# Gathers and sums of a graph network: GpSimd's memsets between gathers, and who clears the banks

## The chip, the cores and the metric

The program runs on one core of one Trainium2 chip. The metric is the time of the program on the device in microseconds; less is better. The core's engines are TensorE (PE in the profile, its weight loads PEld), VectorE (DVE), ScalarE (ACT), GpSimd (POOL) and SyncE (SP). Each runs its own stream of instructions, and they meet at semaphores.

## The reference

12500 nodes with 128 features, 212500 edges sorted by destination, each with one of 8 relations. Two relational layers and a third, plain one sum messages over the edges:

```python
def _rgcn_layer(x, W, SW, b, src, dst, rel):
    xt = jnp.einsum('nd,rde->rne', x, W)
    msg = xt[rel, src]
    agg = jax.ops.segment_sum(msg, dst, num_segments=x.shape[0])
    return jax.nn.relu(agg + x @ SW + b)
...
deg = jax.ops.segment_sum(jnp.ones_like(dst, dtype=jnp.float32), dst, num_segments=N)
d_invsqrt = jnp.maximum(deg, 1.0) ** (-0.5)
feat = jax.nn.relu(x @ W1 + b1)
h = feat * d_invsqrt
agg = jax.ops.segment_sum(h[src], dst, num_segments=N)
feat = feat - agg * d_invsqrt
return feat @ W2 + b2
```

Between the layers stand a residual and a layer norm over the features, and another pair at the end. All values are float32.

## The kernel before

Three sums over all edges follow each other: r1 gathers rows of x, r2 rows of x1 (the output of the first layer), r3 rows of h. The edges lie in 1661 **tiles** of 128. For each tile, one indirect DMA on GpSimd's queue (line 794) gathers the 128 source rows of 512 bytes into a slot of `rows`. A one-hot matrix S made by VectorE (line 1042 in r1 and r2, 1235 in r3) says to which of a window's destinations (and, in r1 and r2, relations) each edge belongs, and TensorE multiplies the tile by it (lines 980 and 1205), adding into a PSUM bank.

7 tiles are a **group** (KG) of 64 destinations, two groups a **pair** (PAIR, 14 tiles), four pairs an **iteration** (RING = 8 groups, 56 tiles). `rows` has 56 slots, so the gathers of a pair wait until TensorE is done with the same pair of the iteration before (semaphore `summed`), and until ScalarE has copied their indices (`idx_ready`, line 738). The rest of an iteration's work is for a chunk of 436 nodes whose sums are complete: the classes Tail1, Tail2 and Tail3 (the dense layers, the norms, loads and stores by SyncE).

**GpSimd** (class Gathers, `run`) issues the gathers in order. Behind each it writes a 128x128 MEMSET into a tile `pause` that nobody reads (line 798). The last MEMSET of every group (r1, r2) or of every pair (r3) increments `paused`, and before the next group's (pair's) first gather GpSimd waits for it (line 788). `gate` increments a semaphore that nobody waits for. The first 14 tiles of r2 and 21 of r3 are gathered early (line 764), while the sum before is being finished; these have no MEMSET.

**TensorE** in r1 and r2 (`tensor` in relational_sum): two banks take groups in turn. Group h waits until ScalarE has copied out group h-2 (`agg_out`), clears the bank with a bfloat16 matmul of zeros over its 512 columns (line 964), and adds its 7 tiles. In r1, before the first group of a pair, the matmuls of line 973 count the edges of each destination: 3 for each group, one for each block of 32 destinations that a window of 64 can touch, into 3 columns of 32 rows. VectorE adds these columns to `found` (line 1093). After the first pair of an iteration stands the mix: 8 matmuls of 512 columns (line 950) that multiply the sums of the iteration before, by relation, by the layer's weights. In r3 a group's first matmul starts its bank anew, and there is neither mix nor clearing.

**ScalarE** (`scalar`) copies the indices of the next iteration, waits for the mix, and copies each group out of its bank (`take_out`, line 904); each copy increments `agg_out`:

```python
act.wait_ge(summed, n + (h + 1 + RING))
act.copy(agg[:, h, :, :], agg_ps[h % BUFS][:, :].rearrange("p (n r) -> p n r", r=NREL)
         ).then_inc(agg_out, 1)
```

**VectorE** makes the one-hots two pairs ahead; in r1 also `hot` and `placed` for the counts (lines 1037 and 1040). It adds the mixed sums into `acc` (line 1081), and runs the chunk's elementwise work.

## Time and profile before

| | us |
|---|---|
| median of 3 runs | 7358.1 |
| lowest and highest of them | 7354.17, 7372.18 |
| span of the profiled execution | 7320.2 |
| GpSimd busy | 5851.5 (80%) |
| TensorE busy, matmuls and weight loads | 3691.2 (50%), 2669.6 (36%) |
| VectorE busy, ScalarE busy | 1720.1 (23%), 409.6 (6%) |

The profile comes from one execution, on the core; its own time is not listed apart from its span, which is 37.9 us under the median of the runs. "Busy" counts the time in which an engine executes; waits, branches and register instructions are not in it. For TensorE the ends of matmuls are modelled, so that its busy share is less sure than that of the others. GpSimd's idle time put down to "issue" is time in which no semaphore held it back by the profile: its sequencer and the start of the next instruction. "remote" is a release that the profile could not match with an instruction. The clock is the share of 2.4 GHz that TensorE was granted: 0.5 is 1.2 GHz.

### The profile page before, as it was taken

The page shows a single profiled execution, that of the slowest core. Times are in us where ns is not written, and L with a number is a line of the kernel's source. Part 1 is how long each engine was busy: PE and PEld are TensorE (multiplying, and loading weights), DVE is VectorE, ACT ScalarE, POOL GpSimd, SP SyncE. Part 2 cuts the span into 40 slices and gives each one's busy share as a digit, 9 for nine tenths or more (in the row PEclk, how much of TensorE's full clock was granted, in tenths as well). Part 3 has the DMA queues.
Part 4 walks back from the last instruction along what each step waited for, and adds up shares of the span by engine and source line. Part 5 has one row for each costly group of instructions (what it writes and reads, how often), then busy time and mean ns, then how long its engine had stood idle before and what let it go on. Part 6 is the DMA issues. An engine that isn't in the chain of part 4 may idle for free.

```text
span 7320.2 us, 56431 instructions
## 1 busy us (share of the span) xinstructions
PE 3691.2 (50%) x13687; PEld 2669.6 (36%) x13841; DVE 1720.1 (23%) x2844; ACT 409.6 (6%) x915; POOL 5851.5 (80%) x9940
## 2 busy tenths in 40 slices
PE   4555555555555556556565555554424333433343
PEld 3333333333333333334343333433323333333333
DVE  4333333333333212222222222221101111111111
ACT  1000000000000100000000000010000000000000
POOL 7888888888888588888888888867888888888887
PEclk7666667676666777767677776675555555555555
DMA  2111111111111112211222221211111111111111
GB/s 66 49 51 52 50 50 50 51 52 50 50 52 51 40 49 57 56 56 55 56 58 56 56 57 56 56 54 42 51 51 52 51 51 51 51 51 53 51 51 48
DMA packets 197585, 382.88 MB, mean 52 GB/s; under 512 B 84322, under 2 KB 93326, under 8 KB 197542
## 3 DMA queue, kind: packets, MB, share of 16 engines
q0 software_dynamic: 159456, 326.88, 17.0%
q1 hardware_dynamic: 36416, 54.67, 2.1%
q10 hardware_dynamic: 1670, 0.85, 0.0%
q8 instruction: 15, 0.25, 0.0%
q14 instruction: 28, 0.23, 0.0%
HBM read 356.43 MB, written 25.65 MB: 52 GB/s over the span
## 4 chain that ended last, share of the span: by engine, by line
POOL 48%; issue 20%; another core or an unknown queue 20%; PE 7%; DVE 3%; DVEq 1%; POOLq 0%; ACT 0%; DMA 0%; ACTq 0%; SPq 0%
POOL rows L794 39%; POOL pause L798 9%; PE bank L980 3%; PE bank L950 3%; DVE r_S L1042 1%; DVE r_hot L1037 1%; PE bank L1205 1%; ACT r_agg L904 0%; PE bank L1440 0%; PE bank L964 0%; DVE acc L1081 0%; DMA acc<-in_dst_dram 0%; DVEq L1071 0%; POOLq L109 0%
## 5 line engine op out<-in xcount | busy, mean ns | idle before, releaser
L794 POOL DMA_INDIRECT rows<-in_x_dram,idx x1661 | 1588.6, 956 | 466.9 <-issue 396.7
L794 POOL DMA_INDIRECT rows<-x_d,idx x1647 | 1574.2, 956 | 453.5 <-issue 397.8
L794 POOL DMA_INDIRECT rows<-h_d,idx x1640 | 1566.9, 955 | 441.4 <-issue 396.3
L980 PE MATMUL bank<-r_S,rows 128*128 128x128 f32 x6644 | 1408.2, 380 | 705.1 <-issue 486.8
L1205 PE MATMUL bank<-r_S,rows 128*128 128x64 f32 x3322 | 821.9, 388 | 1332.3 <-issue 1079.4
L980 PEld LDWEIGHTS bank<-r_S,rows 128*128 128x128 f32 x6644 | 1299.5, 285 | 501.4 <-issue 482.1
L1205 PEld LDWEIGHTS bank<-r_S,rows 128*128 128x128 f32 x3322 | 775.1, 315 | 1378.0 <-issue 1272.4
L798 POOL MEMSET pause<- 128x128 f32 x4948 | 1096.3, 222 | 4.3 <-issue 0.2
L1042 DVE TENSOR_TENSOR r_S<-bank,key 128x1792 f32<-128x1792 f32 x238 | 480.4, 2019 | 1225.9 <-remote 1080.3
L964 PEld LDWEIGHTS bank<-zeros_bf 128*128 128x128 bf16 x476 | 54.1, 114 | 1463.0 <-issue 1056.8
L964 PE MATMUL bank<-zeros_bf 128*128 128x512 bf16 x323 | 174.9, 542 | 722.4 <-issue 505.8
L904 ACT COPY r_agg<-bank 128x512 f32<-128x512 f32 x476 | 272.1, 586 | 4257.1 <-remote 3286.7
L1262 DVE TENSOR_TENSOR acc<-acc,bank 128x64 f32 x238 | 52.8, 222 | 1877.3 <-remote 1561.9
L1037 DVE TENSOR_TENSOR r_hot<-bank,b_spot 128x1344 bf16<-128x1344 f32 x119 | 185.4, 1558 | 1223.4 <-remote 1051.5
L950 PE MATMUL bank<-r_agg,w1s 128*128 128x512 f32 (+1 forms) x528 | 459.7, 1036 | 14.3 <-issue 12.7
L950 PE MATMUL bank<-r_agg,w2s 128*128 128x512 f32 (+1 forms) x528 | 458.7, 1035 | 3.7 <-issue 2.0
L1040 DVE TENSOR_REDUCE r_placed<-r_hot 128x192 bf16<-128x1344 bf16 x119 | 289.9, 2436 | 4.1
L950 PEld LDWEIGHTS bank<-r_agg,w1s 128*128 128x128 f32 x528 | 121.9, 234 | 327.2 <-issue 326.3
L950 PEld LDWEIGHTS bank<-r_agg,w2s 128*128 128x128 f32 x528 | 118.3, 225 | 316.4 <-issue 315.4
L1081 DVE TENSOR_TENSOR acc<-acc,bank 128x64 f32 x492 | 109.2, 222 | 406.5 <-PE bank L950 182.7
L973 PE MATMUL bank<-one_bf,r_placed 128*32 128x1 bf16 x714 | 37.5, 168 | 310.5 <-issue 187.3
L1235 DVE TENSOR_TENSOR r_S<-bank,key 128x896 f32<-128x896 f32 x119 | 129.8, 1092 | 35.9 <-DVE acc L1262 22.2
(152 smaller groups left out, 1471.1 us busy)
## 6 DMA issues: line engine op xcount, KB each, us to landing
rows<-in_x_dram,idx POOLq DMA_INDIRECT x1661, 3.3
rows<-x_d,idx POOLq DMA_INDIRECT x1647, 3.4
rows<-h_d,idx POOLq DMA_INDIRECT x1640, 3.4
d_xr<-in_x_dram SPq DMA_DIRECT2D x54, 218.0 KB
x_d<-d_yr SPq DMA_DIRECT2D x27, 218.0 KB
d_x1r<-x_d SPq DMA_DIRECT2D x27, 218.0 KB
h_d<-d_hr SPq DMA_DIRECT2D x27, 218.0 KB
part_d<-d_pr SPq DMA_DIRECT2D x27, 218.0 KB
```

The source lines that it names most:

```text
L794: pool.indirect_dma_start(out=self.c.rows[:, self.place(s), :], out_offset=None, in_=self.table[:, :], in_offset=bass.IndirectOffsetOnAxis ...
L798: ins = pool.memset(self.c.pause[:, s % PT, :], 0.0)
L904: act.copy(agg[:, h, :, :], agg_ps[h % BUFS][:, :].rearrange("p (n r) -> p n r", r=NREL)).then_inc(agg_out, 1)
L950: mm = pe.matmul(mix_ps[:, 0:groups * GN], W[:, r, :], agg[:, first:first + groups, :, r], start=(r == 0), stop=(r == NREL - 1))
L964: pe.matmul(agg_ps[j][:, :], c.zeros_bf[:, :], c.zeros, start=True, stop=False, skip_group_check=True)
L980: mm = pe.matmul(agg_ps[j][:, bass.ds(offs[j * KG + k], TK)], c.rows[:, g.place(h * KG + k), :], S[:, pb, j * KG + k, :], start=False, sto ...
L1037: ch.then(dve.tensor_tensor(hot[:, b, :, :], spots.unsqueeze(1).broadcast_to([P, PT, SPOTS]), bc_last(blocks.spot[:, at], SPOTS), ALU.is_e ...
L1040: dve.tensor_reduce(placed[:, b, :, :], hot[:, b, :, :].rearrange("p (j k) n -> p j n k", k=KG), AX.X, ALU.add)
L1042: dve.tensor_tensor(S[:, b, :, :], c.iota[:, :].unsqueeze(1).broadcast_to([P, PT, TK]), bc_last(c.key[:, at], TK), ALU.is_equal).then_inc( ...
L1081: ins = dve.tensor_tensor(window, window, mix_ps[:, w * GN:(w + 1) * GN], ALU.add)
L1205: mm = pe.matmul(sum_ps[b][:, j * GN:(j + 1) * GN], c.rows[:, g.place(h * KG + k), :], S[:, b, j * KG + k, :], start=(k == 0), stop=(k == ...
L1235: dve.tensor_tensor(S[:, p % BUFS, :, :], c.iota[:, 0:GN].unsqueeze(1).broadcast_to([P, PT, GN]), bc_last(c.key[:, bass.ds(i * UN + p * PT ...
```

## The change

On **GpSimd**, the MEMSETs, the tile `pause`, the semaphore `paused` and the waits for it go. In their place `breathe` waits, before some pairs, until the group issued just before has landed: in the first iteration of a sum before pairs 1, 2 and 3, later before pairs 0 and 2 (r1, r2) or pair 0 alone (r3). On **ScalarE**, each copy out now increments `taken`; ScalarE waits for it, writes zeros into the bank and increments `agg_out` with that. **TensorE** no longer clears, and counts a group with one matmul over all 96 spots, into one column; `found` gets 96 rows, **VectorE** adds one column of 96 rows where there were 3 of 32, and Tail2 puts the three blocks of `found` together with 12 matmuls where 4 transposes stood.

```diff
-        self.rest = PAIR if then is None else 1
+        self.rests = (0,) if then is None else (0, PR // 2)
...
+    def breathe(self, pool, i, p):
+        pool.wait_ge(self.landed[p * PAIR - 1 if p else RING - 1], (i + 1 if p else i) * (KG * 16))
+        gate(pool, self.c.passed)
...
+                if p > 0 if first else p in self.rests:
+                    self.breathe(pool, i, p)
                 for h in range(p * PAIR, (p + 1) * PAIR):
-                    if h % rest == 0:
-                        pool.wait_ge(self.paused, q * (NG // rest) + i * (RING // rest) + h // rest + 1)
-                        gate(pool, self.c.passed)
                     for k in range(part.of(h)):
...
                         pool.indirect_dma_start(
...
                         ).then_inc(self.landed[slot], 16)
-                        ins = pool.memset(self.c.pause[:, s % PT, :], 0.0)
-                    if h % rest == rest - 1:
-                        ins.then_inc(self.paused, 1)
...
+        for b in range(BUFS):
+            zero(act, c, agg_ps[b][:, :]).then_inc(agg_out, 1)
...
                     act.copy(agg[:, h, :, :], agg_ps[h % BUFS][:, :].rearrange("p (n r) -> p n r", r=NREL)
-                             ).then_inc(agg_out, 1)
+                             ).then_inc(taken, 1)
+                    act.wait_ge(taken, n + (h + 1))
+                    zero(act, c, agg_ps[h % BUFS][:, :]).then_inc(agg_out, 1)
...
                     pe.wait_ge(agg_out, n + (h + 1))
-                    pe.matmul(agg_ps[j][:, :], c.zeros_bf[:, :], c.zeros, start=True, stop=False,
-                              skip_group_check=True)
...
                             for of in range(PAIR):
-                                for b in range(COLS):
-                                    at = of * COLS + b
-                                    mm = pe.matmul(cnt_ps[:, at:at + 1],
-                                                   placed[:, pb, of, b * NODES:(b + 1) * NODES], c.one_bf[:, :],
-                                                   start=True, stop=True)
+                                mm = pe.matmul(cnt_ps[:, of:of + 1], placed[:, pb, of, :], c.one_bf[:, :],
+                                               start=True, stop=True)
...
-                        window = c.found[:, bass.ds(blocks_at[first + j], COLS)]
-                        ins = dve.tensor_tensor(window, window, cnt_ps[:, j * COLS:(j + 1) * COLS], ALU.add)
+                        window = c.found[:, bass.ds(blocks_at[first + j] + (COLS - 1), 1)]
+                        ins = dve.tensor_tensor(window, window, cnt_ps[:, j:j + 1], ALU.add)
```

GpSimd's stream inside the loop of r1, before: the start of an iteration, its second group, and the start of its second pair.

```order
L780 ISA [waits r1_idx_ready]
L788 REGISTER_ALU [waits r1_summed]
L794 DMA rows<-in_x_dram,idx 128x128 [waits r1_paused]
L798 MEMSET pause 128x128
...
L798 MEMSET pause 128x128
L794 DMA rows<-in_x_dram,idx 128x128 [waits r1_paused]
L798 MEMSET pause 128x128
...
L779 REGISTER_ALU
L780 REGISTER_ALU [waits r1_idx_ready]
L788 REGISTER_ALU [waits r1_summed]
L794 DMA rows<-in_x_dram,idx 128x128 [waits r1_paused]
```

And with the change, from the start of an iteration (pair 0) to that of its third pair:

```order
L780 ISA [waits r1_idx_ready]
L769 REGISTER_ALU [waits r1_summed]
L789 DMA rows<-in_x_dram,idx 128x128 [waits r1_landed7]
L789 DMA rows<-in_x_dram,idx 128x128 x13
L779 REGISTER_ALU
L780 REGISTER_ALU [waits r1_idx_ready]
L789 DMA rows<-in_x_dram,idx 128x128 [waits r1_summed]
L789 DMA rows<-in_x_dram,idx 128x128 x13
L779 REGISTER_ALU
L780 REGISTER_ALU [waits r1_idx_ready]
L769 ISA [waits r1_summed]
L789 DMA rows<-in_x_dram,idx 128x128 [waits r1_landed3]
```

The MEMSETs and their semaphore are gone; at pairs 0 and 2 a wait for landed rows stands ahead of the first gather.

ScalarE in r1, copying groups out, before:

```order
L904 COPY r_agg<-bank 128x512
L903 REGISTER_ALU
L904 COPY r_agg<-bank 128x512
L903 REGISTER_ALU
L904 COPY r_agg<-bank 128x512
```

And with the change:

```order
L896 COPY r_agg<-bank 128x512
L898 REGISTER_ALU
L576 CAST bank<-zeros_bf 128x512
L895 REGISTER_ALU
L896 COPY r_agg<-bank 128x512
L898 REGISTER_ALU
```

Each copy is now followed by one that writes zeros into the same bank.

TensorE in r1, from the end of the mix to the first tile of the second pair, before:

```order
L956 TENSOR_LOAD off_i
L963 REGISTER_ALU
L964 MATMUL bank<-zeros_bf 128x512
L967 REGISTER_ALU
L973 MATMUL bank<-one_bf,r_placed 32x1 x6
L980 ISA
```

And with the change:

```order
L950 TENSOR_LOAD off_i
L957 REGISTER_ALU
L959 REGISTER_ALU
L963 MATMUL bank<-one_bf,r_placed 96x1 x2
L969 ISA
L969 MATMUL bank<-r_S,rows 128x128
```

The clearing is gone and six count matmuls have become two.

## Rows read from the trace of the kernel before

**Rows 1.** The page: its busy line, and the chain's shares by line
```profile
PE 3691.2 (50%) x13687; PEld 2669.6 (36%) x13841; DVE 1720.1 (23%) x2844; ACT 409.6 (6%) x915; POOL 5851.5 (80%) x9940
...
POOL rows L794 39%; POOL pause L798 9%; PE bank L980 3%; PE bank L950 3%; DVE r_S L1042 1%; DVE r_hot L1037 1%; PE bank L1205 1%; ACT r_agg L904 0%; PE bank L1440 0%; PE bank L964 0%; DVE acc L1081 0%; DMA acc<-in_dst_dram 0%; DVEq L1071 0%; POOLq L109 0%
```

**Rows 2.** The page, groups of instructions: the gathers and their memset
```profile
L794 POOL DMA_INDIRECT rows<-in_x_dram,idx x1661 | 1588.6, 956 | 466.9 <-issue 396.7
L794 POOL DMA_INDIRECT rows<-x_d,idx x1647 | 1574.2, 956 | 453.5 <-issue 397.8
L794 POOL DMA_INDIRECT rows<-h_d,idx x1640 | 1566.9, 955 | 441.4 <-issue 396.3
...
L798 POOL MEMSET pause<- 128x128 f32 x4948 | 1096.3, 222 | 4.3 <-issue 0.2
```

**Rows 3.** Table by stretches, one for each sum (start:end and length, then busy times)
```profile
core 0: us, PE busy (x) PEld busy (x) DVE busy (x) ACT busy (x) POOL busy (x), PEclk, DMA share, GB/s
4.50:2422.30 2417.80, 1325.00 (x4926) 863.30 (x5013) 859.67 (x958) 178.33 (x362) 1952.16 (x3321) 0.69 0.19 52
2466.80:4874.10 2407.30, 1400.55 (x4851) 918.10 (x4912) 515.95 (x960) 182.50 (x388) 1948.48 (x3306) 0.71 0.20 56
4902.10:7297.50 2395.40, 897.75 (x3646) 838.66 (x3646) 314.63 (x836) 43.16 (x151) 1946.31 (x3300) 0.51 0.19 51
```

**Rows 4.** Chains of waits of 100:2400, 2500:4850 and 5000:7280 us, by line
```profile
by line: another core or an unknown queue 55.7%; issue 16.3%; PE bank L980 8.2%; PE bank L950 6.4%; DVE r_S L1042 4.0%; DVE r_hot L1037 2.0%; PE bank L964 0.7%; ACT r_agg L904 0.7%; PE bank L1440 0.7%; DVEq L1071 0.6%; DVE acc L1081 0.5%; D
...
by line: POOL rows L794 61.3%; issue 22.1%; POOL pause L798 15.0%; another core or an unknown queue 0.3%; POOLq L109 0.2%; PE bank L950 0.2%; PE bank L980 0.2%; POOLq L780 0.2%; POOLq L788 0.2%; DMA rows<-x_d,idx 0.1%; PE bank L1570 0.1%; P
...
by line: POOL rows L794 60.3%; issue 20.5%; POOL pause L798 14.2%; another core or an unknown queue 3.8%; PE bank L1205 0.9%; POOLq L109 0.3%; POOLq L779 0.1%; PE bank L1726 0.1%; DMA rows<-h_d,idx 0.1%; POOLq L804 0.0%; DVE d_o L1781 0.0%;
```

**Rows 5.** Waits in the same stretches: GpSimd's in sum 1, TensorE's in 2, 3
```profile
POOL rows L794 <- remote: 20.8, 13, 2.6
...
PE bank L980 <- DMA rows<-x_d,idx: 176.3, 39, 8.9
...
PE bank L1205 <- DMA rows<-h_d,idx: 195.6, 45, 10.4
```

**Rows 6.** Timeline at the end of sum 1: the last gather, ScalarE's next and last copy
```profile
2422.25 0.95 POOL L794 DMA_INDIRECT rows<-in_x_dram,idx  x1 [0.17 <-issue]
...
2447.95 0.58 ACT L904 COPY r_agg<-bank 128x512 f32<-128x512 f32 x1 [33.95 <-PE bank L980]
...
2481.02 0.58 ACT L904 COPY r_agg<-bank 128x512 f32<-128x512 f32 x1 [1.57 <-remote]
```

**Rows 7.** Timeline of GpSimd in sum 1: one group and the start of the next
```profile
1026.46 0.95 POOL L794 DMA_INDIRECT rows<-in_x_dram,idx  x1 [0.81 <-issue]
1027.41 0.22 POOL L798 MEMSET pause<- 128x128 f32 x1
1027.80 0.95 POOL L794 DMA_INDIRECT rows<-in_x_dram,idx  x1 [0.17 <-issue]
...
1036.47 0.95 POOL L794 DMA_INDIRECT rows<-in_x_dram,idx  x1 [0.81 <-issue]
```

**Rows 8.** Timeline of GpSimd: the first and the last two of 14 early gathers
```profile
2466.80 0.95 POOL L764 DMA_INDIRECT rows<-x_d,e_idx  x1 [43.37 <-SPq L1432]
...
2481.82 0.95 POOL L764 DMA_INDIRECT rows<-x_d,e_idx  x1 [0.31 <-issue]
2483.07 0.94 POOL L764 DMA_INDIRECT rows<-x_d,e_idx  x1 [0.30 <-issue]
```

**Rows 9.** The gathers' own view, line 794: issue to landing
```profile
DMA to landing us min/median/max: 3.3/3.4/3.4
```

**Rows 10.** The clearing in 100:2400; six count matmuls; ScalarE's copies out
```profile
L964 PE MATMUL bank<-zeros_bf 128*128 128x512 bf16 x142 | 79.4, 559 | 447.7 <-issue 309.0 <-ACT r_agg L904 138.6
...
1012.33 0.32 PE L973 MATMUL bank<-one_bf,r_placed 128*32 128x1 bf16 x6
...
L904 ACT COPY r_agg<-bank 128x512 f32<-128x512 f32 x476 | 272.1, 586 | 4257.1 <-remote 3286.7
```

More of the change, by code:

```diff
@@ L153, in build @@
         c.step_t, c.step_g, c.carry = sb("step_t", [P, 1]), sb("step_g", [P, 1]), sb("carry", [P, 1])
-        c.pause = sb("pause", [P, PT, P])
-        c.found = sb("found", [NODES, DEG_COLS + COLS])
+        c.found = sb("found", [SPOTS, DEG_COLS + COLS])
         c.deg = sb("deg", [DEG_ROWS, DEG_PARTS, NODES])
@@ L707, in __init__ @@
         self.cleared = sem("cleared")
-        self.paused = sem("paused")
         self.idx_ready = sem("idx_ready")
@@ L767, in early, with iteration @@
             ).then_inc(then.landed[t // KG], 16)
+    def breathe(self, pool, i, p):
+        pool.wait_ge(self.landed[p * PAIR - 1 if p else RING - 1], (i + 1 if p else i) * (KG * 16))
+        gate(pool, self.c.passed)
     def run(self, pool, ready, stored):
-        rest = self.rest
-        def iteration(q, i, part, set_of, skip=0):
+        def iteration(q, i, part, set_of, skip=0, first=False):
             at = set_of * UN
@@ L776, in iteration @@
                 if (p + 1) * PT <= skip:
-                    pool.sem_inc(self.paused, PAIR // rest)
                     continue
@@ L781, in iteration @@
                 gate(pool, self.c.passed)
+                if p > 0 if first else p in self.rests:
+                    self.breathe(pool, i, p)
                 for h in range(p * PAIR, (p + 1) * PAIR):
-                    if (h + 1) * KG <= skip:
-                        if h % rest == rest - 1:
-                            pool.sem_inc(self.paused, 1)
-                        continue
-                    if h % rest == 0:
-                        pool.wait_ge(self.paused, q * (NG // rest) + i * (RING // rest) + h // rest + 1)
-                        gate(pool, self.c.passed)
                     for k in range(part.of(h)):
@@ L797, in iteration @@
                         ).then_inc(self.landed[slot], 16)
-                        ins = pool.memset(self.c.pause[:, s % PT, :], 0.0)
-                    if h % rest == rest - 1:
-                        ins.then_inc(self.paused, 1)
         def one_round(q, skip=0):
-            iteration(q, 0, FULL, 0, skip)
+            iteration(q, 0, FULL, 0, skip, True)
             with pool.Fori(0, IT // SETS) as n:
@@ L811, in run @@
         pool.sem_inc(self.cleared, 1)
-        pool.sem_inc(self.paused, 1)
         one_round(0, EARLY[self.turns])
@@ L828, in run @@
         pool.end_ifs()
-        pool.wait_ge(self.paused, rounds * (NG // rest) + 1)
-        gate(pool, self.c.passed)
         if self.then is not None:
@@ L864, in relational_sum @@
     agg_out = sem("agg_out")
+    taken = sem("taken")
     mixed = sem("mixed")
@@ L871, in relational_sum @@
     zeroed, zeros = prologue.zeroed if prologue else sem("zeroed"), 2
[L872 removed]
+    agg_ps, mix_ps, cnt_ps = c.psum[0:2], c.psum[2], c.psum[5][0:SPOTS, 0:PAIR]
     NIT = 1 + IT + ENDS
@@ L1617, in start_pe @@
         for b in range(DEG_PARTS):
-            mm = pe.transpose(self.PD[:, b * NODES:(b + 1) * NODES], c.found[:, b * DEG_ROWS:(b + 1) * DEG_ROWS],
-                              c.ident[0:NODES, 0:NODES])
+            for o in range(COLS):
+                at = b * DEG_ROWS + COLS - 1 - o
+                mm = pe.matmul(self.PD[:, b * NODES:(b + 1) * NODES], c.found[:, at:at + DEG_ROWS],
+                               c.ident[0:SPOTS, o * NODES:(o + 1) * NODES], start=(o == 0), stop=(o == COLS - 1))
         mm.then_inc(self.degs_turned, 1)
```

3 lines of the change are left out of this document (removed).

## Prediction

> **What bounds the kernel now.** I read the page first. GpSimd is busy 80% of the span, and line 794, the gathers, holds 39% of the chain that ended last; TensorE is busy 50% [rows 1]. The groups of GpSimd's instructions say how its time is filled: in the first sum 1661 gathers of 956 ns, the pause MEMSET of 222 ns behind each, and 467 us of idle time, almost all of it "issue", its own pace [rows 2]. So GpSimd works without a break, and it would be easy to stop here and credit the whole of a shorter GpSimd stream.
>
> The table by stretches gives the three sums their lengths: 2417.8, 2407.3 and 2395.4 us [rows 3]. A sum has 1661 tiles, 29.66 iterations of 56, so an iteration takes 81.5, 81.2 and 80.8 us. Then I asked each sum for its own chain of waits [rows 4]. Sums 2 and 3 run through GpSimd. Sum 1 does not: its chain goes through TensorE's matmuls, VectorE's one-hots and ScalarE's copies. The waits agree [rows 5]: TensorE waits for landed rows 176 us in sum 2 and 196 us in sum 3, and the same view of sum 1 has no such row; GpSimd in its turn waits there for others a little. And when GpSimd has issued the last gather of sum 1, at 2422.3, ScalarE still has six groups to copy out, the next at 2447.95 and the last at 2481.02 [rows 6]. TensorE is some three pairs behind its rows at the end of sum 1 and has not caught up. The "50% busy" hides that, since the ends of matmuls are modelled.
>
> So there are two sides with nearly one pace. **GpSimd's side**, gathers, memsets and its own idle time, is (1588.6 + 1661 x 0.222 + 396.7 + 44.4) / 29.66 = 80.9 us an iteration in sum 1, and by the same sum, over 1647 and 1640 gathers, 81.1 and 80.0 in sums 2 and 3 [rows 2]. **TensorE's side** (with its handshakes) is the full 81.5 in sum 1; in sum 2 it is 81.2 less the share of landing waits, 176.3 of 2350 us, 75.1; in sum 3 80.8 less 195.6 of 2280, 73.9 [rows 3, 5].
>
> **The change, part by part.**
>
> *The memsets.* Gather, memset, gather has a pitch of 1.34 us [rows 7]. The early gathers, which have no memset, have 1.25: 13 steps in 16.27 us, with 0.30 us idle where the memset lay [rows 8]. So 222 ns of memset are worth only 0.087 us each: 56 x 0.087 = 4.9 us an iteration. That a run of 14 or 21 gathers goes on like this for 1661 is my assumption; the bounds are 0 and 56 x 0.222 = 12.4, and the nearest row is this one.
>
> *The waits on "paused".* Before the first gather of a group the gap is 0.81 instead of 0.17 us [rows 7], 0.64 each: 8 an iteration in sums 1 and 2 (5.1 us), 4 in sum 3 (2.6 us). The waits for indices and freed slots stay; where they are already met the sequencer passes them while a gather runs, so I cost them at nothing. If that cover failed, the rest of the 0.64 would come back at 4 places.
>
> *The waits for landings.* breathe() waits for the gather issued just before, so the queue drains: 61 times in sums 1 and 2 each (2 an iteration), 32 in sum 3 (1). Behind the waiting GpSimd stands the next pair's gathers, and TensorE waits for those, a pair or two later. From issue to landing is 3.3 to 3.4 us in the few gathers that the view can match [rows 9]; start to start is then 3.4 to 3.4 + 0.64 instead of 1.25, a cost of 2.15 to 2.8 us. I take 2.45: 4.9 us an iteration, 2.45 in sum 3. At worst a rest costs what the longest wait for landed rows was, 10.4 us; at best nothing.
>
> The Trainium skill, "DMA: Bandwidth & Descriptors", section on the anatomy of a DMA on the GpSimd path, fits about 2.0 us plus bytes over 436 GB/s, which for the 64 KB of a tile is 2.15 us. By that estimate a rest costs about 1.2 us less and GpSimd's side is 2.5 us an iteration shorter. The row above speaks for more.
>
> GpSimd's side after: 80.9 - 4.9 - 5.1 + 4.9 = **75.8**, 81.1 - 5.1 = **76.0**, 80.0 - 4.9 - 2.6 + 2.5 = **75.0**.
>
> *The clearing of the banks.* TensorE loses 8 matmuls of 559 ns an iteration in sums 1 and 2, 4.5 us, and 4 of 6 count matmuls in each pair of sum 1; six went in 0.32 us, so some 0.4 us an iteration [rows 10]. ScalarE gains 8 copies of about the 585 ns of its copy out (409.6 us busy becomes some 690, still under 10%). With two banks, group h needs the clearing that follows group h-2, and while ScalarE copies and clears (1.2 us) TensorE has group h-1 to do: hidden. Once an iteration it is not: after the mix, where copies and TensorE both stood still, the order is copy, clear, matmul as before, only on another engine. That one is not saved, and I deduct 0.4 more for its semaphores: 4.9 - 0.6 - 0.4 = 3.9 in sum 1, 3.5 in sum 2, 0 in sum 3, which never cleared by matmul. The bounds are 0 (each matmul stood where TensorE would wait) and 4.9; I am near the upper, since in sum 1 TensorE never waits for rows.
>
> TensorE's side after: 81.5 - 3.9 = **77.6**, 75.1 - 3.5 = **71.6**, **73.9**.
>
> *found in 96 rows, its turn in 12 matmuls instead of 4 transposes*: once a program, under 5 us, taken as nothing.
>
> **The sum.** The slower side decides, plus what two sides of nearly one pace cost each other; before that was 0.6, 0.1 and 0.8 us an iteration (81.5 against 80.9 and so on). Sum 1: 77.6 + 0.6 = 78.2. Sum 2: 76.0 + 0.4 = 76.4. Sum 3: 75.0 + 1.5 = 76.5, as its sides are now 1.1 apart and it had the larger loss. Saved: (3.3 + 4.8 + 4.3) x 29.66 = 368 us. The profiled span is 7320.2, so 6952; the median of the runs is 37.9 us higher and I take the saving from it: 7358.1 - 368 = **6990 us**. What is late next: in sum 1 TensorE's chain, in sums 2 and 3 GpSimd with its gathers.
>
> **Rivals.**
>
> A. *GpSimd's side alone decides*, because TensorE's side gives way (its clock, at 0.69 of full, has room to rise [rows 3]). 75.8, 76.0, 75.0: (5.7 + 5.2 + 5.8) x 29.66 = 495, so 6863. For it: GpSimd is the chain of sums 2 and 3 [rows 4]. Against it, for sum 1: [rows 5, 6].
>
> B. *TensorE's side caps it*: the clearings were cheap where they stood and sum 1 stays at 81.5; sum 2 comes to 77.5, sum 3 to 78.5. (0 + 3.7 + 2.3) x 29.66 = 178, so 7180. For it: part of the idle time before line 964 is a wait for ScalarE's copy, which stays [rows 10].
>
> C. *Slower: TensorE's clock.* The granted clock is 0.69 and 0.71 in sums 1 and 2, a mix of the levels 1.2 and 2.4 GHz, and 0.51 in sum 3, where TensorE has neither the mix nor the 512-column clearings [rows 3]. Taking 512-column matmuls out and putting a wait for ScalarE in might let it fall to, say, 0.58. TensorE's side would be 77.6 x 0.69 / 0.58 = 92.3 and 71.6 x 0.71 / 0.58 = 87.6, with sum 3 at 76.5: (10.8 + 6.4 - 4.3) x 29.66 = 383 longer, 7741. It decides below a mean of about 0.62, where 53.5 / c + 50.8 / c passes 167 us. Against it: the 8 wide mix matmuls of each iteration stay. The Trainium skill, "TensorE: Matmul & The Clock Gate", section on the second failure mode, describes a kernel whose cycling through banks left short idle times between groups and made the clock swing between its two levels; the swinging is here already.
>
> D. *The pitch does not fall*: gathers in long runs take 1.34 us without a memset too, because something else sets it. GpSimd's side is 80.7, 80.9 and 79.9, the rests eat what the waits gave, and the time is some 7345: no change. For it: only runs of 14 and 21 show 1.25.
>
> **How the numbers follow.** Forecast 0.57, A 0.16, B 0.12, C 0.10, D 0.05. About 0.3% (22 us) is what a measurement of this kernel can tell from no change. Forecast, A and B are faster: 0.85. D is the same: 0.05. C is slower: 0.10. The range leaves out C and D and the far tails of A and B: 6800 to 7230. A rest that costs 1 us more or less moves GpSimd's side by 154 us in all, of which TensorE's side hides a part in sum 1; the range holds that too.
>
> **What would show each step.** Right: line 794's successor with a pitch of 1.25 us and 0.30 idle in runs of 14; gaps of 3.4 to 4.1 us between starts, twice an iteration; sum 1 at about 2320 us with its last copies still some 50 us behind the last gather and its chain through TensorE; sums 2 and 3 at about 2270. Wrong: a pitch of 1.34 (D), or gathers that are themselves longer than 956 ns; rests of 5 us and more; the granted clock of sums 1 and 2 under 0.62 (C); sum 1 unchanged while GpSimd waits for freed slots (B), or all sums at GpSimd's own pace (A).

## Result: slower by 1.4%, and what the profile after shows

The change took 7457.0 us (median of 4 runs, 7447.0 to 7485.6) beside 7356.1 us for the kernel before (4 runs, 7339.6 to 7372.2): ratio 1.0142, 95% interval 1.0117 to 1.0167. The forecast was 6990 and the range ended at 7230. One thing is needed to follow the numbers below: the kernel before itself took 7137 to 7138 us in three later groups of runs and 7232 and 7336 us in two others, each group on one chip, so every number below is compared only inside its own group. I call the first three **free**, and the other two and the first pair **held**, for a reason that the traces give.

The page of the change: busy line and chain that ended last.

```profile
PE 3315.2 (44%) x12908; PEld 2433.6 (33%) x12909; DVE 1715.9 (23%) x2844; ACT 688.1 (9%) x1395; POOL 4726.3 (63%) x4992
...
another core or an unknown queue 24%; issue 17%; PE 10%; POOL 2%; DVE 2%; DVEq 1%; ACT 1%; ACTq 0%; DMA 0%; POOLq 0%
```

GpSimd went from 80% to 63% busy and from nearly half of the chain [rows 1] to 2% of it. The work left it as intended, and the time did not. The 24% under "another core or an unknown queue" can't be taken at its word, since the program runs on one core; what that name hides comes below.

The table by stretches, the three sums (compare [rows 3]):

```profile
core 0: us, PE busy (x) PEld busy (x) DVE busy (x) ACT busy (x) POOL busy (x), PEclk, DMA share, GB/s
4.50:2468.20 2463.70, 1163.72 (x4320) 761.28 (x4321) 860.02 (x958) 315.61 (x596) 1575.08 (x1661) 0.65 0.19 51
2509.30:4998.00 2488.70, 1208.23 (x4634) 785.39 (x4633) 506.20 (x949) 316.70 (x622) 1570.91 (x1660) 0.70 0.19 54
5059.30:7456.90 2397.60, 854.09 (x3646) 827.73 (x3646) 315.17 (x836) 43.78 (x152) 1576.35 (x1660) 0.51 0.19 51
```

Sums 1 and 2 became 46 and 81 us longer, sum 3 stayed, though GpSimd has some 375 us less to execute in each. GpSimd's timeline shows that the pitch fell as forecast, from 1.34 us [rows 7] to 1.25; the next two views are GpSimd's waits in 100:2400, sum 1 (us in total, times, longest), and the start of a pair in its timeline:

```profile
POOL rows L789 <- remote: 225.0, 47, 6.5
POOL rows L789 <- PE bank L969: 68.0, 13, 13.6
```

```profile
1027.12 0.95 POOL L789 DMA_INDIRECT rows<-in_x_dram,idx  x1 [3.44 <-remote]
1028.38 0.95 POOL L789 DMA_INDIRECT rows<-in_x_dram,idx  x1 [0.30 <-issue]
1029.63 0.95 POOL L789 DMA_INDIRECT rows<-in_x_dram,idx  x1 [0.30 <-issue]
```

It issues faster and then stands at pair starts, waiting for slots that TensorE has not freed: 225 + 68 us, where the same stretch before had 20.8 us under "remote" [rows 5]. So TensorE's side holds all three sums. In sum 3, where the change alters nothing on TensorE, its timeline shows what that side looks like:

```profile
6028.07 0.95 POOL L789 DMA_INDIRECT rows<-h_d,idx  x1 [0.30 <-issue]
6028.37 0.29 PEld L1193 LDWEIGHTS bank<-r_S,rows 128*128 128x128 f32 x1 [2.51 <-issue]
6029.32 0.95 POOL L789 DMA_INDIRECT rows<-h_d,idx  x1 [0.30 <-issue]
6029.77 0.26 PE L1193 MATMUL bank<-r_S,rows 128*128 128x64 f32 x1 [2.54 <-issue]
6030.57 0.94 POOL L789 DMA_INDIRECT rows<-h_d,idx  x1 [0.30 <-issue]
6031.17 0.29 PEld L1193 LDWEIGHTS bank<-r_S,rows 128*128 128x128 f32 x1 [2.51 <-issue]
6031.82 0.94 POOL L789 DMA_INDIRECT rows<-h_d,idx  x1 [0.30 <-issue]
6032.57 0.26 PE L1193 MATMUL bank<-r_S,rows 128*128 128x64 f32 x1 [2.54 <-issue]
...
6037.47 0.29 PEld L1193 LDWEIGHTS bank<-r_S,rows 128*128 128x128 f32 x1 [1.11 <-issue]
6037.48 0.47 PE L1193 MATMUL bank<-r_S,rows 128*128 128x64 f32 x1 [0.43 <-issue]
6038.17 0.29 PEld L1193 LDWEIGHTS bank<-r_S,rows 128*128 128x128 f32 x1 [0.41 <-issue]
6038.18 0.47 PE L1193 MATMUL bank<-r_S,rows 128*128 128x64 f32 x1 [0.23 <-issue]
...
6039.58 1.96 PE L1193 MATMUL bank<-r_S,rows 128*128 128x64 f32 x8 [0.24 <-issue]
...
6040.61 0.94 POOL L789 DMA_INDIRECT rows<-h_d,idx  x1 [7.85 <-issue]
```

Read the starts. A weight load or a matmul of 0.26 to 0.29 us starts every 1.40 us: 6028.37, 6029.77, 6031.17, 6032.57. A group is 14 such matmuls, and by the kernel TensorE waits for rows before its first tile and at most once more inside it, so most of these steps have no semaphore in front of them. Some 4 us after GpSimd's last gather (6031.82) the steps shrink to 0.70 us (6037.47, 6038.17, each with its matmul), and then eight matmuls go in 1.96 us. The group done, slots come free and GpSimd starts again at 6040.61.

In sums 1 and 2 the time is lost at another place. TensorE's and ScalarE's timelines in sum 1, and the same work in e5, a later run of the same kernel:

```profile
1012.79 4.84 PE L969 MATMUL bank<-r_S,rows 128*128 128x128 f32 x28
...
1026.21 0.29 PE L963 MATMUL bank<-one_bf,r_placed 128*96 128x1 bf16 x2 [7.79 <-ACT bank L576]
```

```profile
1024.77 0.59 ACT L896 COPY r_agg<-bank 128x512 f32<-128x512 f32 x1 [11.26 <-remote]
1025.38 0.59 ACT L576 CAST bank<-zeros_bf 128x512 f32<-128x512 bf16 x1
```

```profile
1026.55 5.02 PE L969 MATMUL bank<-r_S,rows 128*128 128x128 f32 x28
...
1028.88 0.59 ACT L896 COPY r_agg<-bank 128x512 f32<-128x512 f32 x1 [1.56 <-PE bank L969]
...
1031.60 0.59 ACT L896 COPY r_agg<-bank 128x512 f32<-128x512 f32 x1 [1.51 <-PE bank L969]
```

28 matmuls are two groups. In e5 ScalarE copies the first one out while the second runs, and the second at 1031.60, as its matmuls end (1031.57). Here both have ended by 1017.63, and ScalarE, idle, starts its first copy at 1024.77, 7 us later; it clears the bank, and only then can TensorE go on, at 1026.21. Counted over the copies of sums 1 and 2 before which ScalarE stood idle (without the two behind each mix), from the start of the group's last matmul to the copy: never over 0.5 us in the traces of e1 to e12, a mean of 7.4 and 8.0 us here, 11.1 and 10.1 us in the trace of before.

### The profile page after: what moved, and what is told of

Its sections match the earlier page's. It is cut to its first block, busy times and chain, and to the rows that moved or that the text cites. A ratio compares the mean times of both kernels' runs of the same rounds, so it can differ in the third digit from the quotient of the medians.

```text
span 7483.8 us, 50404 instructions
## 1 busy us (share of the span) xinstructions
PE 3315.2 (44%) x12908; PEld 2433.6 (33%) x12909; DVE 1715.9 (23%) x2844; ACT 688.1 (9%) x1395; POOL 4726.3 (63%) x4992
## 4 chain that ended last, share of the span: by engine, by line
another core or an unknown queue 24%; issue 17%; PE 10%; POOL 2%; DVE 2%; DVEq 1%; ACT 1%; ACTq 0%; DMA 0%; POOLq 0%
PE bank L1193 4%; PE bank L944 2%; PE bank L969 2%; POOL rows L789 2%; PE bank L1716 0%; ACT r_agg L896 0%; PE bank L1558 0%; DVE acc L1250 0%; PE bank L1583 0%; PE bank L1572 0%; DVE d_st L1759 0%; PE bank L1579 0%; DVE acc L1069 0%; DVE d_o L1771 0%
## 5 line engine op out<-in xcount | busy, mean ns | idle before, releaser
L789 POOL DMA_INDIRECT rows<-x_d,idx x1647 | 1558.6, 946 | 913.9 <-issue 541.0
L969 PE MATMUL bank<-r_S,rows 128*128 128x128 f32 x6644 | 1191.5, 350 | 1097.0 <-issue 558.4
L969 PEld LDWEIGHTS bank<-r_S,rows 128*128 128x128 f32 x6644 | 1119.8, 261 | 1192.2 <-issue 1190.8
L1193 PE MATMUL bank<-r_S,rows 128*128 128x64 f32 x3322 | 779.2, 390 | 1404.6 <-issue 1293.3
L1193 PEld LDWEIGHTS bank<-r_S,rows 128*128 128x128 f32 x3322 | 764.0, 320 | 1426.3 <-issue 1368.2
L944 PE MATMUL bank<-r_agg,w1s 128*128 128x512 f32 (+1 forms) x528 | 483.6, 1030 | 245.8 <-issue 237.5
L963 PE MATMUL bank<-one_bf,r_placed 128*96 128x1 bf16 x238 | 31.4, 201 | 781.2 <-ACT bank L576 562.8
L963 PEld LDWEIGHTS bank<-one_bf,r_placed 128*96 128x96 bf16 x238 | 25.5, 155 | 846.1 <-issue 842.4
L576 ACT CAST bank<-zeros_bf 128x512 f32<-128x512 bf16 x480 | 282.2, 588 | 15.2
L735 ACT COPY idx<-src_i x360 | 71.4, 203 | 1040.3 <-remote 685.7
```

The costliest lines, as they stand in the source:

```text
L576: return act.copy(ap, c.zeros_bf[0:ap.shape[0], 0:1].broadcast_to([*ap.shape]))
L735: act.copy(self.c.idx[:, bass.ds(at, PT)], self.c.src_i[:, bass.ds(i * UN + p * PT, PT)]).then_inc(self.idx_ready, 1)
L789: pool.indirect_dma_start(out=self.c.rows[:, self.place(s), :], out_offset=None, in_=self.table[:, :], in_offset=bass.IndirectOffsetOnAxis ...
L944: mm = pe.matmul(mix_ps[:, 0:groups * GN], W[:, r, :], agg[:, first:first + groups, :, r], start=(r == 0), stop=(r == NREL - 1))
L969: mm = pe.matmul(agg_ps[j][:, bass.ds(offs[j * KG + k], TK)], c.rows[:, g.place(h * KG + k), :], S[:, pb, j * KG + k, :], start=False, sto ...
L1193: mm = pe.matmul(sum_ps[b][:, j * GN:(j + 1) * GN], c.rows[:, g.place(h * KG + k), :], S[:, b, j * KG + k, :], start=(k == 0), stop=(k == ...
```

## The experiments

Eighteen runs in five groups. "Before" stands for the kernel before in the same group.

### Group 1 (free; before 7138.3 us): the change in parts

e1, GpSimd's part alone, on the kernel before:

```diff
+                if p > 0 if first else p in self.rests:
+                    self.breathe(pool, i, p)
...
-                        ins = pool.memset(self.c.pause[:, s % PT, :], 0.0)
-                    if h % rest == rest - 1:
-                        ins.then_inc(self.paused, 1)
```

> The kernel before with the GpSimd part of the change alone: no MEMSETs, no waits for them, the waits for landed rows. TensorE clears the banks and counts as before. Theory 1 (the hand-over of a bank: ScalarE's clearing lengthens the way from a group's last matmul to the group after next by about 0.65 us, and that way is what paces TensorE in sums 1 and 2): this part is a gain by itself, 50 to 250 us, 7110 to 7310. Theory 2 (the rests: each drains the queue, TensorE gets its rows in bursts, and the slack between the two sides is lost): this part alone is already slower, 7400 to 7500. Theory 3 (the clock: without the 512-column clearings TensorE is granted less): as theory 1, with the clock of sums 1 and 2 at 0.68 and 0.71.

e2, ScalarE's clearing alone:

```diff
+                    act.wait_ge(taken, n + (h + 1))
+                    zero(act, c, agg_ps[h % BUFS][:, :]).then_inc(agg_out, 1)
...
-                    pe.matmul(agg_ps[j][:, :], c.zeros_bf[:, :], c.zeros, start=True, stop=False,
```

> The kernel before with ScalarE's clearing alone; MEMSETs, their waits and the six count matmuls stay. Theory 1: slower by 100 to 250 us, 7460 to 7610, all of it in sums 1 and 2, with the clock near 0.68 and 0.71. Theory 2: no slower than before, 7250 to 7360. Theory 3: slower too, but with the granted clock of sums 1 and 2 at 0.65 or less.

e3, the change with TensorE's clearing put back and ScalarE's taken out (e2's edit reversed):

> The whole change but for ScalarE's clearing: TensorE clears the banks as before. It is the run before last plus the count in one matmul. Theory 1 and theory 3: faster than the kernel before by 60 to 270 us, and some 10 to 20 us under the run with the GpSimd part alone. Theory 2: about the time of the change, 7400 to 7500.

e4, both clear (e2 without its last line):

> The kernel before with ScalarE's clearing added and TensorE's kept, so that each bank is cleared twice. Theory 1: the longer way and TensorE's matmuls both count, at least as slow as ScalarE's clearing alone and up to 120 us slower, 7460 to 7700. Theory 3: the 512-column matmuls are there, so the clock and the time are those of before, 7340 to 7400. Theory 2: as before, 7340 to 7400.

Measured: e1 6664.2, ratio 0.9337 (0.9322 to 0.9353). e2 7137.2, 0.9998 (0.9988 to 1.0008). e3 6665.7, 0.9339 (0.9323 to 0.9354). e4 7138.1, 1.0000 (0.9990 to 1.0009). So here GpSimd's part gives 474 us, and who clears, and how often, is worth nothing, nor are the counts (e3 against e1). That contradicts the first pair, so the change itself had to run again.

### Group 2 (free; before 7137.2 us): the change again, rests, a doubled clearing

e5 is the change unaltered.

> The change itself, beside the kernel before and the parts of it on one chip. Bank hand-over (T1: with the clearing on ScalarE, TensorE's next group waits for copy, semaphore and clearing, some 0.65 us more a group than with its own matmul): slower than the change with TensorE's clearing kept (6665.7 us on the chip of the first experiments) wherever TensorE's side sets the pace; if the handshake shows fully, 8 x 0.65 x 59.3 iterations less the 0.56 matmuls, 40 to 300 us more, 6700 to 6960 us. GpSimd alone decides (T0: on this chip TensorE has slack and the clearing is covered wherever it stands): 6650 to 6680 us, ratio to before 0.934. Clock (T3: without the 512-column clearings it falls under 0.62): 7000 us and more, with a granted clock under 0.62 in the first two sums.

e6 is e1 without the waits for landings:

```diff
-                if p > 0 if first else p in self.rests:
-                    self.breathe(pool, i, p)
```

> The kernel before with GpSimd's part alone, and without the waits for landings too: the gathers stand behind each other with only the waits for indices and freed slots. If a rest costs what my sum says, 2.45 us each (154 of them), 377 us less than GpSimd's part with the rests (6664.2 us): 6290 us as far as TensorE's side lets it, else down to TensorE's own pace, 6400 to 6550. If the rests keep the queue from something worse (a full queue that stops GpSimd in the midst of a gather), the gathers' own busy time grows past 956 ns and the time is 6664 us or more.

e7 doubles the hand-over's suspected cost (`twice` is n + n):

```diff
-                    act.wait_ge(taken, n + (h + 1))
+                    act.wait_ge(taken, twice + (2 * h + 1))
+                    zero(act, c, agg_ps[h % BUFS][:, :]).then_inc(taken, 1)
+                    act.wait_ge(taken, twice + (2 * h + 2))
                     zero(act, c, agg_ps[h % BUFS][:, :]).then_inc(agg_out, 1)
```

> The change with ScalarE clearing each bank of the first two sums twice, with a semaphore between: a group's hand-over is longer by one clearing of 0.588 us and one semaphore, some 0.65 us. T1: each of the 8 hand-overs of an iteration shows, 5.2 us x 59.3 iterations, 310 us above the change. T0: two banks in turn cover it and the time is within 20 us of the change's. In between: only the hand-over behind the mix shows, 0.65 x 2 banks x 59.3, 40 to 80 us.

e8 is e3 again:

> The change with TensorE's clearing kept, a second time, so that the change itself and this stand beside each other on one chip. T1: faster than the change by 40 to 300 us. T0: within 20 us of the change, both at 0.934 of before. Should this be a chip on which the kernel before takes some 7350 us, as in the first profile, where TensorE was behind its rows all through sum 1, T1 says 7100 to 7250 here against 7457 for the change; T0 says both alike.

Measured: e5 6668.9, ratio 0.9344 (0.9328 to 0.9359). e6 6283.0, 0.8804 (0.8789 to 0.8818). e7 6668.8, 0.9344 (0.9328 to 0.9360). e8 6664.2, 0.9338 (0.9322 to 0.9353). **The same change is 6.6% faster here**, and a doubled clearing costs nothing. The profile of e5, its chain, sum 1 and 3 by stretches, its waits, and TensorE's timeline in sum 3:

```profile
POOL 65%; issue 24%; DMA 7%; PE 3%; DVE 1%; POOLq 1%; ACT 0%; SPq 0%; DVEq 0%; ACTq 0%
```

```profile
4.50:2220.50 2216.00, 1215.56 (x4400) 819.01 (x4400) 863.27 (x976) 319.84 (x600) 1569.36 (x1660) 0.70 0.21 56
...
4507.30:6654.00 2146.70, 839.77 (x3691) 792.49 (x3691) 319.37 (x857) 44.56 (x154) 1571.08 (x1661) 0.51 0.21 57
```

```profile
PE bank L1193 <- DMA rows<-h_d,idx: 1290.2, 233, 8.7
PE bank L969 <- DMA rows<-in_x_dram,idx: 886.6, 140, 10.1
...
POOL rows L789 <- DMA rows<-x_d,idx: 191.4, 60, 5.1
POOL rows L789 <- DMA rows<-in_x_dram,idx: 147.7, 61, 5.9
POOL rows L789 <- DMA rows<-h_d,idx: 73.4, 31, 2.5
```

```profile
5502.02 3.22 PE L1193 MATMUL bank<-r_S,rows 128*128 128x64 f32 x14 [7.66 <-DMA rows<-h_d,idx]
```

A group's 14 matmuls go through in 3.22 us while gathers run at the same 1.25 us pitch as in the first pair. TensorE waits 887 us for rows in sum 1 and 1290 us in sum 3. Now the same line of the same kernel in the first pair:

```profile
PE bank L1193 <- issue: 1293.3, 768, 10.5
```

Much the same idle time in all, but cut otherwise: 233 waits of 5.5 us on average when free, 768 of 1.7 us when held. And the wait for a cleared bank in sum 1 (100:2400), in the first pair's run of the change and in e5:

```profile
PE bank L963 <- ACT bank L576: 553.2, 49, 37.6
```

```profile
PE bank L963 <- ACT bank L576: 45.3, 29, 1.6
```

These two, short idle times inside the groups of sum 3 and late hand-overs of banks in sums 1 and 2, are the difference between free and held.

**What the held traces lack.** The names of the releasers can't carry this comparison, for they come from recorded semaphore events, and held traces lack most of these. A gather raises its semaphore 16 times, so 4983 gathers make 79728 landing events. Each trace of e1 to e12 has 80468 to 80579 of them, with those of other transfers. The trace of before has 21541, the change 16159, and e13 to e18 have 16305, 17712, 33405, 20957, 14940 and 20775. So a wait under "issue", "remote" or "another core or an unknown queue" in a held trace may be one whose release was not recorded, and a row of waits for landed rows is a lower bound there. Starts of instructions don't suffer from this: the tile matmuls, 6644 in sums 1 and 2 and 3322 in sum 3, are in every trace. The transfers themselves are no slower: the 79728 packets of 4096 bytes take 0.24 us on average in the traces of before, the change and e5 alike.

e6 prices the rests: 6664.2 - 6283.0 = 381 us over 154 rests, 2.47 us each. The rows of e5's waits above agree: 191.4 + 147.7 + 73.4 = 412.5 us in 152 of them, 2.71 each, less the 0.30 that stands before any gather. They are not alike: 2.4 us each in sums 1 and 3, 3.2 in sum 2.

### Group 3 (free; before 7138.1 us): TensorE made the slower side by real work

In e9, e10 and e11 (before, the change, and the change with TensorE's clearing) four matmuls of zeros stand before each tile's matmul in sums 1 and 2; e12 is the change without its rests:

```diff
+                        for _ in range(4):
+                            pe.matmul(agg_ps[j][:, :], c.zeros_bf[:, :], c.zeros, start=False, stop=False,
+                                      skip_group_check=True)
```

> The kernel before, with TensorE made the slower side in the first two sums: before each tile's matmul four bfloat16 matmuls add zeros over the 512 columns of the bank (in the third sum nothing is added). At 0.21 us each at full clock that is 48 us an iteration on top of TensorE's own work, some 85 to 95 us in all against GpSimd's 80: I expect 7137 us plus 5 to 15 us for each of 59.3 iterations, 7450 to 8050. It is the base for the two runs beside it. If TensorE still has slack, 7137 to 7160.

> The change with the same four zero matmuls before each tile of the first two sums. The bank hand-over makes the change slow (T1) where TensorE is the slower side: 50 to 300 us above the same load with TensorE's own clearing (e11), and in the first two sums no shorter than before with the load, as in the first pair of profiles. My sum for the prediction (3.9 and 3.5 us less an iteration on TensorE's side): 150 to 220 us under e11. In both cases the third sum is some 140 us shorter than before's, since it has no load. If neither shows, this and e11 agree within 20 us, and what made the change slower in the first pair of profiles is nothing that a longer TensorE stream brings out.

> The change with TensorE's clearing kept and the same load. Against before with the load only GpSimd's part, the counts and the third sum differ: with TensorE the slower side, the first two sums are as long as before's loaded ones within 1% and the third some 140 us shorter, so 120 to 200 us under e9. If the waits for landings hurt when TensorE is behind (T2), the first two sums are longer than in e9.

> The change as it stands, without its waits for landings. T0 (GpSimd alone decides, the clearing is covered): 6283 us within 15, as GpSimd's part without them had. T1: at a pitch of 70 us an iteration TensorE's side is nearer, and the hand-over now shows: 6320 to 6500. Should this be a chip on which before takes some 7350 us, T2 (the rests cost there too) says 7300 or less, and a TensorE that is simply slower there says 7400 to 7480, as the change itself.

Measured: e9 7375.9, ratio 1.0333 (1.0316 to 1.0351). e10 7164.4, 1.0037 (1.0023 to 1.0052). e11 7191.1, 1.0072 (1.0055 to 1.0089). e12 6281.8, 0.8800 (0.8785 to 0.8815), the fastest of all, 12% under before. The stretches of e10 and then of e11, sums 1 and 2:

```profile
4.50:2409.40 2404.90, 2295.36 (x10608) 1290.46 (x10813) 847.83 (x955) 316.17 (x595) 1570.06 (x1660) 0.98 0.19 52
2471.40:4914.10 2442.70, 2361.99 (x10964) 1349.31 (x11195) 499.08 (x946) 322.17 (x624) 1567.20 (x1660) 0.99 0.20 55
```

```profile
4.50:2422.00 2417.50, 2332.19 (x10833) 1308.33 (x11039) 847.87 (x954) 178.48 (x361) 1571.75 (x1661) 0.99 0.19 52
2486.30:4944.90 2458.60, 2404.29 (x11220) 1368.89 (x11426) 499.10 (x946) 182.43 (x387) 1569.45 (x1661) 0.99 0.20 54
```

With TensorE truly the bound (81 to 83 us an iteration, as in the first pair), moving the clearing to ScalarE gains 12.6 and 15.9 us a sum. My sum for the prediction gave 116 and 104; the hand-over theory, a loss. Neither came, with one reservation: the load also raised the granted clock to 0.98 and 0.99, from 0.65 to 0.71 in the first pair, so that the clearing taken away was a shorter one (383 ns in e11's trace) than the 559 ns of my sum. And the loaded change stays under the loaded before by 211 us. 165 of them are sum 3, which has no load (2325.3 against 2160.2); but the loaded sums 1 and 2 are shorter too, by 35 and 14 us, where in the first pair they grew by 46 and 81. A long TensorE stream alone is not what was seen there.

### Group 4 (held; before 7232.1 us): the change and GpSimd's part

e13 is the change, e14 is e1 again, both unaltered.

> The change itself, on whatever chip this comes to. Where the kernel before takes 7138 us, as in the three groups of runs so far: 6650 to 6680. Where it takes some 7350, as beside the first profile: 7440 to 7490, with TensorE's instructions in steps of 0.7 us in the third sum, where neither kernel changes anything on TensorE. A mixture (before at 7138 and the change at 7400 or more) would say that the change itself brings the slow TensorE about.

> GpSimd's part alone, beside the change. Where before takes 7138 us: 6664 within 5, as the change. Where it takes some 7350: if a slow TensorE sets the pace there whatever the kernel asks, 7300 to 7450; if the clearing on ScalarE is what makes the change slow there, under 7250.

Measured: e13 7387.4, ratio 1.0208 (1.0191 to 1.0225); e14 7408.6, 1.0246 (1.0229 to 1.0263). The slow result repeats, and **GpSimd's part alone is enough for it**; the rest of the change takes 21 us off. Sum 1 and 3 of e14:

```profile
4.50:2451.10 2446.60, 1233.19 (x5017) 758.38 (x5018) 860.65 (x958) 176.02 (x362) 1576.04 (x1660) 0.69 0.19 51
...
4990.70:7369.90 2379.20, 838.02 (x3650) 803.87 (x3649) 315.19 (x836) 43.92 (x152) 1576.58 (x1660) 0.51 0.19 51
```

The clock is 0.69 and 0.51, that of [rows 3], so it isn't the clock either. ScalarE's copies are late here too, by 6.9 and 9.7 us on average in sums 1 and 2.

### Group 5 (held; before 7336.5 us): what of GpSimd's part

This group ran on the chip of group 2, where before had taken 7137: held is not a property of the chip alone.

e15, before with the waits for landings added, memsets kept (e1's two added lines only):

> The kernel before, with its memsets and their waits, and the waits for landings added. Where before takes 7138 us and GpSimd alone decides, 154 waits at my 2.45 us come on top: 7515 (by the pair of runs with and without them 2.47 each, 7519); less if they cover part of the waits for the memsets at the same places, 93 x 0.64 = 60 us, so 7420 to 7520. Where a slow TensorE sets the pace (before 7230 to 7360): if the waits for landings are what made the change slow there, 100 us and more above before; if the missing memsets are, within 50 us of before.

e16, before with one wait for memsets a pair:

```diff
-        self.rest = PAIR if then is None else 1
+        self.rest = PAIR
```

> The kernel before, waiting for its memsets once a pair in all three sums as it does in the third: 4 waits fewer an iteration in the first two sums. By my 0.64 us each that is 2.6 x 59.3 = 152 us less where GpSimd decides, 6986 of 7138. Nothing if the gap belongs to the start of a group whatever is waited for. Where a slow TensorE sets the pace: within 50 us of before.

e17 is e6 again, e18 is e2 again:

> GpSimd's part without the waits for landings. Where before takes 7138 us: 6283, as before. Where a slow TensorE sets the pace and GpSimd's part made it slower (7408 beside 7232): if the waits for landings did it, below before, under 7230; if gathers at a pitch of 1.25 us, without memsets between, slow TensorE down, 7300 and more.

> The kernel before with the clearing on ScalarE alone. Where before takes 7138 us: the same within 10. Where a slow TensorE sets the pace: if each TensorE instruction costs time there, 20 to 200 us under before, since 476 clearings go; if the hand-over of the banks costs, 50 us and more above before.

Measured: e15 7421.2, ratio 1.0118 (1.0101 to 1.0135). e16 7396.5, 1.0078 (1.0061 to 1.0096). e17 7473.4, 1.0186 (1.0169 to 1.0203). e18 7350.3, 1.0013 (0.9998 to 1.0027). The kernel that was 12% faster when free (e6) is the slowest of this group. What lets GpSimd issue faster (e16 a little, e17 most) makes the kernel slower. The rests aren't needed for it, since e17 has none; what they add to it was not tried inside one group. e18's clearing is again within the measurement. Waits of TensorE, of e17 over the program, of e16 in sum 1, and of e15 over the program:

```profile
PE bank L1193 <- issue: 1354.7, 774, 10.3
```

```profile
PE bank L980 <- issue: 318.5, 297, 3.6
```

```profile
PE bank L1214 <- DMA rows<-h_d,idx: 1038.0, 172, 11.4
PE bank L989 <- DMA rows<-in_x_dram,idx: 1027.3, 161, 11.0
```

e15 is the surprise. It is slower because GpSimd is (its sum 1 takes 2494 us), but TensorE waits at least 1027 us for rows in that sum: its own side was at most 2494 - 1027 = 1467 us, 49 an iteration. In e16, same chip and group, with gathers only slightly denser than before's, TensorE is behind its rows all through a 2442 us sum 1. That can be read without any releaser. From the start of a group's last gather to the start of its first matmul it takes 5.0 us at the median in e15's sum 1, as in e1 to e8 (5.0 to 5.4), and 44 us in e16's. And from the last gather of sum 1 to the first early gather of sum 2, which waits for what the sum stores, it is 4.6 us in e15 and 46.5 in e16 (44.5 in before's trace, 41.1 in the change's, 6.5 in e5). e15 is not quite free: its copies come 4.1 and 2.1 us late, and 33405 landing events are less than half. So TensorE's pace in a held run depends on how GpSimd issues.

## Why the prediction was wrong

**What was right.** *The memsets* and *the waits on "paused"*: the pitch is 1.25 us, and in group 2 both together without rests (e6) gave 854 us; my terms, 4.9 three times and 5.1 + 5.1 + 2.6 over 29.66 iterations, make 816. *The rests*: 2.45 us each forecast, 2.47 measured (381 / 154). That is in part luck: I had one landing time, 3.4 us, from the few gathers of a held trace; e5's view has 2.5 us in sums 1 and 3 and 3.5 in sum 2, and the rests differ with it. The Trainium skill, "DMA: Bandwidth & Descriptors", section on the anatomy of a DMA on the GpSimd path, gives 2.15 us to land as an estimate by its fit; the traces are above it, and the 1.2 us less for a rest is not borne out. *found in 96 rows*: nothing (e3 against e1). Where runs were free the change came to 0.934 of before, 468 us less, beside 495 of rival A. It was sum 1's TensorE bound that I weighed against A, and in free runs there is none.

**The step that failed** is "TensorE's side (with its handshakes) is the full 81.5 in sum 1", and 75.1 and 73.9 in the others, taken as a length of TensorE's own work that stays put when GpSimd changes, and shrinks when an instruction is taken out. Free runs show the work itself: in e5's sum 1, 2216 - 887 us of waits for rows, over 29.66, is 45 us an iteration. The other 37 us of my 81.5 were not TensorE's work: in sums 1 and 2 mostly banks handed over late, in sum 3 steps between instructions. (The deductions for sums 2 and 3 were unsafe besides: they came from waits for landed rows in a trace with 21541 of some 80500 landing events.) And that time grows when GpSimd's gathers come closer: TensorE's side became (2463.7 / 29.66) 83.1 and 83.9 us in sums 1 and 2 instead of 77.6 and 71.6, and 80.8 in sum 3 instead of 73.9.

The marks were in the trace. One is the 55.7% of sum 1's chain under "another core or an unknown queue" [rows 4], in a program on one core: I read the chain past it, through TensorE. In e4, before with a second clearing and free, that name is gone, and POOL has 76% of the chain. The other is in the waits of before, sum 3's tile matmul:

```profile
PE bank L1205 <- issue: 1079.4, 918, 9.8
PE bank L1205 <- DMA rows<-h_d,idx: 195.6, 45, 10.4
```

I quoted the second line [rows 5] and deducted its 196 us. The first says that short matmuls stood idle 1079 us, 1.2 us at a time, for no reason that the profile names. Before's timeline shows the same grid, with memsets between the gathers:

```profile
5722.93 0.29 PEld L1205 LDWEIGHTS bank<-r_S,rows 128*128 128x128 f32 x1 [1.13 <-issue]
5722.95 0.46 PE L1205 MATMUL bank<-r_S,rows 128*128 128x64 f32 x1 [0.96 <-issue]
...
5724.36 0.29 PEld L1205 LDWEIGHTS bank<-r_S,rows 128*128 128x128 f32 x1 [1.14 <-issue]
5724.39 0.45 PE L1205 MATMUL bank<-r_S,rows 128*128 128x64 f32 x1 [0.98 <-issue]
```

Here two instructions go every 1.4 us, where after the change it was often one. Counted over the starts of weight loads and matmuls between 5200 and 6600 us, steps of 0.70 and of 1.40 us (each within 0.05): before 477 and 231, the change 295 and 384, e14 278 and 397, e17 315 and 470, e15 245 and 79; in e1 to e12 none of either. What they cost shows in the time from the first to the last of a group's 14 matmuls in sum 3: a mean of 2.82 us in every one of e1 to e12, 6.96 in before, 7.72 in the change, 6.96 in e14, 8.08 in e17, 3.94 in e15. Eight groups an iteration make 8 x (6.96 - 2.82) = 33 us of before's 80.8. In sums 1 and 2 such steps are there too, but the larger part lies at the hand-over: of TensorE's idle time in 100:2200, 516 of 861 us in before and 829 of 1053 in the change lie ahead of an instruction that waits for `agg_out`, the bank given back by ScalarE; in e5 it is 38 of 926.

*The clearing* was mis-sized: 3.9 and 3.5 us an iteration forecast where TensorE bounds, (12.6 + 15.9) / 59.3 = 0.5 measured in group 3, at nearly full clock. At the clock of the first pair only held runs tell, and they say no more: in group 4 the change is 21 us under GpSimd's part alone, 0.4 an iteration, and in group 5 the clearing alone is within the measurement. That the copy, semaphore and clearing in a row take back most of what TensorE saves is my explanation and was not tried by itself.

**The rivals.** B came nearest in kind: sum 1 unchanged while GpSimd waits for freed slots. But B let sums 2 and 3 gain; TensorE's side there rose with GpSimd's pace and swallowed all of it. C had the sign (slower, 0.10) with the wrong mechanism: the granted clock is 0.65, 0.70 and 0.51, above its bound of 0.62, and e14, which keeps the clearings on TensorE, is as slow at 0.69. D fell with the pitch.

**What is shown and what is not.** Shown: that in held runs TensorE's instructions in sum 3 come in steps of 0.70 and 1.40 us, inside groups too, and that in sums 1 and 2 ScalarE starts its copies many us after a group's last matmul; that both are absent in the free traces, also at the densest gathers (e12) and with more than twice the matmuls (e10); that in held groups faster issue on GpSimd makes the kernel slower (e14, e16, e17) and slower issue gives TensorE most of its pace back (e15, in sums 1 and 2). The order within a stretch (steps of 1.40 beside gathers, 0.70 and less once they stop) fits a resource that gathers and TensorE's instructions share, but what that resource is was not tried; nor is it known why a group is held, since one chip was seen both ways. Whether a copy is late because its signal is, or because the matmuls really end later than the profile models, is open too. One rival stands untested: held traces are also those that lack most semaphore events, and every time here is of an execution that was recorded for its span and clock, so the recording may have a part in the slowness and not only in the gaps. The 101 to 177 us by which the change, e14 and e17 lie above before in their groups are measured; how much of them each slow stretch makes is not.

## What to carry to other kernels

Idle time put down to "issue" between short matmuls is not the engine's own work: before costing an edit by "this engine's side", take that idle time out and ask whether it would be there with its neighbour quieter. Ask also whether the trace can name a releaser at all: compare its landing events with those that the program must make, and be warned by "another core" in a program on one core. Where they are missing, go by the starts of instructions, as from a group's last matmul to its copy. A margin of one per cent between two sides is no forecast when one of them moves with the other. And when a result contradicts its trace's arithmetic, run the unchanged kernels again in another group before explaining it: here the same change is 0.934 of before or 1.02 of it, and the version without rests 0.88 or 1.019.

## What the runs showed of the hardware

- TensorE's instructions can come one per 0.70 or 1.40 us for stretches of tens of us (6006 to 6037 in the change), inside groups where the kernel has no wait; its granted clock (0.51 there) does not tell it, for e5 shows 0.51 too and 14 matmuls in 3.22 us.
- In the same runs ScalarE's copy of a finished bank starts 7 to 15 us after the group's last matmul on average (the change, before, e14, e16, e17), where it starts within 0.5 us in e1 to e12.
- Those runs' traces keep 14940 to 33405 of some 80500 landing events, while every gather packet is there and takes its 0.24 us.
- A kernel's time can differ between groups of runs by 2.8% (7137 and 7336 us, same chip) while inside a group runs of one kernel lie within 0.1 to 0.6% of each other.
- A 222 ns memset in the shade of a gather adds 0.09 us to the pitch (1.34 against 1.25). In held runs its going, together with the waits on "paused", is a loss (137 us, e17); by itself it was not tried.
- A wait for the last gather's landing costs 2.47 us where GpSimd bounds (154 of them, 381 us).
